# Local attention: which engine reads the projected rows first, and what stands behind it in each queue

## The chip, the cores and the metric

One Trainium2 chip, one of its cores. The metric is the device time of one execution in microseconds (us), smaller is better. The engines are TensorE (PE, with its weight loads as PEld), VectorE (DVE), ScalarE (ACT), GpSimd (POOL) and SyncE (SP). Each takes its instructions in the order of its own queue, and waits for the others on semaphores.

## The reference, cut to what matters

The whole program is two layers of a small network over 16 sequences of 256 tokens with 128 features: linear attention, experts, a retention block, and last a stack of two local attention layers, each with a feed-forward part. The change touches the local attention alone:

```python
h = shift_token(x)
q, k, v = jnp.split(h @ wqkv, 3, axis=-1)          # 8 heads of 64
q = l2norm(q) * qs;  k = l2norm(k) * ksc
q, k = rotary_xpos(q, k)                           # each row times cos and sin tables
sim = jnp.einsum('bhwid,bhwjd->bhwij', bq * 8.0, bk)   # windows of 64, looking one window back
sim = jnp.where(mask, -jnp.finfo(sim.dtype).max, sim)
attn = jax.nn.softmax(sim, axis=-1)
out = jnp.einsum('bhwij,bhwjd->bhwid', attn, bv)
x = x + out @ wo
```

## The kernel before, in words

`local_layer` is called twice. Its attention part works on eight chunks of 512 tokens (two sequences), each of four tiles of 128 tokens. A *step* holds four tiles of projection for chunk g, most of the scores and values of chunk g - 1, and the last ones with the output product of chunk g - 2. A step has eight *blocks*, `blk` 0 to 7, and every engine walks through the same blocks in an order written out by hand in its own `step` function. The first step of a layer only projects, the second projects and attends, six do all three, and two more drain. The six run as three rounds of a hardware loop of two steps.

In an even block, for tile t:

- PE, `project_qk` (L1410): q into bank BA and k into bank BB, three matmuls each. It waits until ACT has copied the turned rows of an earlier tile out of the same two banks (`qk_r`).
- ACT, `squares` (L1561): the squares of both banks into `sq`. DVE, `rotate` (L1664): both banks times the tables, into `R`. DVE waits for the squares of a bank before it reads that bank, so ACT always reads first and DVE last, and `rotated` is the semaphore that tells PE that a bank may be overwritten.
- DVE, `lengths` (L1671, L1674): row sums of `sq`, clipped. ACT, `norms` (L1566, L1569), the last thing in ACT's even block: logarithm and exponential of the sums, the reciprocal lengths `rn`.
- POOL (L1385, L1392): adds the two halves of the rotation and multiplies by `rn`. 

In an odd block PE projects v into BA (L1419) and turns the rows of the tile before (`turn`, L1436) into BB and BA. ACT copies v (`keep_values`, L1590), and later the turned rows (`keep_rows`, L1577 and L1584).

Every block also carries one pair of heads through four stages, each a block or two behind the other: `maxima_scores` on PE (L1450, L1454) and `maxima` on DVE (L1683, L1685); `scores` with `less_maxima` (L1471 to L1486) and ACT's `weights` (L1601); `weighted_values` (L1498, L1499); ACT's `denominators` (L1607, L1609) and DVE's `normalise` (L1694). `maxima_scores` may overwrite its banks only when DVE has read the pair before (`max_r`). Twice in a step, in blocks 2 and 6, PE turns the collected maxima (L1505), ACT copies them (`maxima_rows`, L1595, tile `mT`), and `less_maxima` waits for the copy; in these two blocks PE issues `maxima_scores` behind `less_maxima`, in the others ahead of `scores`. In block 4 PE forms the output product of chunk g - 2 in bank BB (`output`, L1515), and in block 6 DVE writes the shifted input rows of the next chunk (`shift_chunk`, L1647 to L1651).

Of the kernel before, what the change touches and what calls it, by code (L numbers as in the profile page):

```python
# [1292 lines left out]
def need(eng, sem, value):  # L1293

    if not isinstance(value, int) or value > 0:
        eng.wait_ge(sem, value)


def local_layer(k, l, shared):
# [5 lines left out]
    with ExitStack() as big:  # L1305
# [4 lines left out]
        with ExitStack() as ctx:  # L1310
# [36 lines left out]
            def staged(g, par, project, attend, finish, blk, lag):  # L1347


                p = blk - lag  # L1350
                if p >= 0:
                    return (g - 1, 1 - par, p) if attend else None
                return (g - 2, par, p + NPAIR) if finish else None
# [43 lines left out]
            def _(pe):  # L1397
                pe.wait_ge(zeroed, 4 * L)

                def project_qk(g, par, t, attend):  # L1400
                    n = NTILE * g + t
                    if not attend:
                        need(pe, rotated, 2 * n)
                        need(pe, v_sb, n)
                    if t == 0:
                        pe.wait_ge(shifted, g + 1 + l)
                    need(pe, qk_r, 2 * n - 2)
                    for qk, bank in enumerate((BA, BB)):
                        for wp, hp in PASSES:
                            m = nc.tensor.matmul(ps[bank][:], hs[hp][par][:, t * P:(t + 1) * P],  # L1410
                                                 k.lw["wqkv"][wp][:, qk * INNER:(qk + 1) * INNER],
                                                 start=(wp + hp == 0), stop=(wp == 1))
                        m.then_inc(proj, 1)

                def project_v(g, par, t):
                    n = NTILE * g + t
                    pe.wait_ge(rotated, 2 * n + 1)
                    for wp, hp in PASSES:
                        m = nc.tensor.matmul(ps[BA][:], hs[hp][par][:, t * P:(t + 1) * P],  # L1419
                                             k.lw["wqkv"][wp][:, 2 * INNER:3 * INNER], start=(wp + hp == 0), stop=(wp == 1))  # L1420
                    m.then_inc(v_mm, 1)

                def turn(c, t, project, written):
                    n = NTILE * c + t
                    for qk, bank in enumerate((BB, BA)):
                        if not project:
                            need(pe, qk_r, 2 * n)
                        elif bank == BA:
                            pe.wait_ge(v_sb, n + 2)
                        elif written is not None:  # L1430
                            pe.wait_ge(resid, written + 1)
                        else:
                            pe.wait_ge(rotated, 2 * n + 4)
                        pe.wait_ge(normed, 2 * n + 1 + qk)
                        for b in range(NB):
                            m = nc.tensor.transpose(ps[bank][:, b * P:(b + 1) * P], R[:, t % 2, qk, 0, b * P:(b + 1) * P],  # L1436
                                                    k.const["ident"][:])
                        m.then_inc(turned, 1)
# [67 lines left out]

                def output(c, par, n):
                    if n is not None:
                        pe.wait_ge(rotated, 2 * n + 2)
                    else:  # L1510
                        pe.wait_ge(qk_r, 2 * NTILE * (c + 1))
                    pe.wait_ge(o_r, NPAIR * (c + 1))
                    pe.wait_ge(w_in, L * 16 * len(names))
                    for b in range(NB):
                        i = nc.tensor.matmul(ps[BB][:], w["wo2"][:, b, :], OT[par][:, b, :], start=(b == 0), stop=(b == NB - 1))  # L1515
                    i.then_inc(x_mm, 1)
# [34 lines left out]
            def _(act):  # L1551
# [4 lines left out]
                def squares(g, t):  # L1556
                    n = NTILE * g + t
                    for qk, bank in enumerate((BA, BB)):
                        act.wait_ge(proj, 2 * n + qk + 1)
                        need(act, clipped, n)  # L1560
                        nc.scalar.activation(sq[:, qk, :], ps[bank][:], ACT.Square).then_inc(squared, 1)  # L1561

# [23 lines left out]
                def keep_values(g, par, t):  # L1586
                    act.wait_ge(v_mm, NTILE * g + t + 1)
                    if t % 2 == 0:
                        need(act, av_mm, NU * (g - 2) + NPAIR * (t // 2 + 1))
                    nc.scalar.activation(VA[par][:, t, :, 0:DH], ps[BA][:].rearrange("p (h d) -> p h d", d=DH),  # L1590
                                         ACT.Copy).then_inc(v_sb, 1)
# [19 lines left out]
                def step(g, par, project, attend, finish):  # L1611
                    now = (g, par, project, attend, finish)
                    for blk in range(2 * NTILE):
                        t = blk // 2
                        if project and blk % 2 == 0:
                            squares(g, t)
                        if project and blk % 2:
                            keep_values(g, par, t)
                        rows = turned_at(g, par, project, attend, blk)
                        if attend and blk in (2, 6):  # L1620
                            maxima_rows(g - 1, blk // 4)
                        dn = staged(*now, blk, 4)
                        if dn:
                            denominators(dn[0], dn[2])
                        sc = staged(*now, blk, 2)
                        if sc:
                            weights(sc[0], sc[2])
                        if blk % 2 and rows:
                            keep_rows(*rows)
                        if project and blk % 2 == 0:  # L1630
                            norms(g, t)
# [4 lines left out]
            def _(dve):  # L1636
# [20 lines left out]
                def rotate(g, t):  # L1657
                    n, i = NTILE * g + t, t % 2
                    for qk, bank in enumerate((BA, BB)):
                        dve.wait_ge(squared, 2 * n + qk + 1)  # L1660
                        need(dve, turned, 2 * n - 3 + qk)
                        x = ps[bank][:].rearrange("p (o h d) -> p o h d", o=1, d=DH).to_broadcast([P, 2, HEADS, DH])
                        y = tab[:, qk, 2 * (t % SPC):2 * (t % SPC) + 2, :].rearrange("p c (o d) -> p c o d", o=1)
                        nc.vector.tensor_tensor(R[:, i, qk, :, :].rearrange("p c (h d) -> p c h d", d=DH), x,  # L1664
                                                y.to_broadcast([P, 2, HEADS, DH]), ALU.mult).then_inc(rotated, 1)

                def lengths(g, t):
                    n, i = NTILE * g + t, t % 2
                    dve.wait_ge(squared, 2 * n + 2)
                    need(dve, rnorm, n - 1)  # L1670
                    nc.vector.tensor_reduce(ss[:, i, :], sq[:].rearrange("p q (h d) -> p (q h) d", d=DH), AX.X,  # L1671
                                            ALU.add).then_inc(sums_r, 1)
                    dve.wait_ge(sums_r, n + 1)
                    nc.vector.tensor_scalar(ss[:, i, :], ss[:, i, :], CLIP2, None, ALU.max).then_inc(clipped, 1)  # L1674
# [37 lines left out]
                def step(g, par, project, attend, finish):  # L1712
                    now = (g, par, project, attend, finish)
                    for blk in range(2 * NTILE):
                        t = blk // 2
                        if project and blk % 2 == 0:
                            rotate(g, t)
                            lengths(g, t)
                        if finish and blk == 5:
                            add_output(g - 2)  # L1720
                        mx = maxima_at(g, project, attend, blk)
                        if mx:
                            maxima(*mx)
                        if attend and blk in (1, 5):
                            split_maxima(g - 1, blk // 4)
                        nr = staged(*now, blk, 4)
                        if nr:
                            normalise(*nr)
                        if project and blk == 6:
                            need(dve, v_mm, NTILE * g)  # L1730
                            shift_chunk(g + 1, 1 - par)
# [242 lines left out]
```

## Time and profile before

| | |
|---|---|
| median of 3 runs | 1837.03 us (1834.8 to 1840.29) |
| the profiled execution's own time | 1841.57 us |
| its span, first to last instruction | 1839.8 us |
| PE busy over the span | 1376.4 us (75%) |
| DVE busy | 1167.5 us (63%) |
| ACT busy | 930.9 us (51%) |
| POOL busy | 723.3 us (39%) |

The span is from the first instruction of the program to the last. Matmuls are pipelined, so busy PE is not PE at its peak. The attention of the first layer runs from 845 to about 1233 us of the span, that of the second from 1341 to 1731 us. The shares are means over stages with different limits; what counts for the change is what each engine waits for inside those two stretches.

### The profile page before, as it was taken

Reading aid. Unit: us, or ns where it says so; the run is one execution under the profiler, and the core shown is the slowest. Engines: PE = TensorE matmul, PEld = TensorE weight load, DVE = VectorE, ACT = ScalarE, POOL = GpSimd, SP = SyncE. Lnnn points to the kernel's source line nnn. Section 1 sums busy time; section 2 is a strip of 40 time slices with the busy share of each in tenths; the row PEclk is TensorE's granted clock in tenths of the full one; section 3 lists DMA queues with packets and bytes.
Section 4 is the critical chain, followed back from the end, with each engine's and each line's share of the span. In section 5 each row is a group of like instructions: output and inputs, shape, how many; then the busy total and the mean of one; then the engine's idle time right before and its main releaser. Section 6 shows DMA issues by size and latency. Waiting matters only on the chain. (4 is left out here: it accounts for less than half of the span.)

```text
span 1839.8 us, 24389 instructions
## 1 busy us (share of the span) xinstructions
PE 1376.4 (75%) x6912; PEld 875.6 (48%) x6912; DVE 1167.5 (63%) x2605; ACT 930.9 (51%) x1749; POOL 723.3 (39%) x588
## 2 busy tenths in 40 slices
PE   7745564674539993874788888888858888889887
PEld 3312121243428872322566666663336666667533
DVE  1598898338448881535777777744467777777444
ACT  6411111344315550563577777764336777777543
POOL 0287787116653664224444333301054444443000
PEclk9867776876769995986899999999958999999999
DMA  5400000012121214000000000000000000000001
GB/s 157 151 0 0 0 0 0 0 47 72 44 62 49 77 47 132 6 0 18 1 1 2 1 1 1 1 26 0 16 2 1 1 2 0 1 0 0 1 0 46
DMA packets 50658, 44.44 MB, mean 24 GB/s; under 512 B 5870, under 2 KB 43763, under 8 KB 50560
## 3 DMA queue, kind: packets, MB, share of 16 engines
q1 hardware_dynamic: 45952, 34.91, 6.5%
q0 software_dynamic: 4608, 8.47, 1.4%
q8 instruction: 32, 0.52, 0.1%
q14 instruction: 66, 0.54, 0.1%
HBM read 23.28 MB, written 21.12 MB: 24 GB/s over the span
## 5 line engine op out<-in xcount | busy, mean ns | idle before, releaser
L1385 POOL TENSOR_TENSOR R<-R 128x512 f32<-128x512 f32 x128 | 159.4, 1267 | 393.6 <-DVE R L1664 393.6
L1664 DVE TENSOR_TENSOR R<-bank,tab 128x1024 f32<-128x1024 f32 x128 | 151.7, 1220 | 138.9 <-ACT sq L1561 133.7
L1392 POOL TENSOR_TENSOR R<-R,rn 128x512 f32<-128x512 f32 x128 | 133.9, 1068 | 12.1 <-issue 10.0
L1498 PE MATMUL bank<-PT,VA 128*128 128x192 f32 x512 | 131.5, 339 | 0.0
L1694 DVE TENSOR_TENSOR OT<-bank,rd 64x256 f32<-64x256 f32 x256 | 106.3, 415 | 18.2 <-ACT rd L1609 16.5
L1034 POOL DMA_INDIRECT expert_rows<-Yt,xin x80 | 82.5, 1031 | 80.2 <-DVE Yt L1007 58.2
L1561 ACT ACTIVATE sq<-bank 128x512 f32<-128x512 f32 x128 | 76.3, 598 | 63.3 <-PE bank L1410 57.4
L1601 ACT ACTIVATE PT<-bank 128x320 f32<-128x320 f32 x256 | 98.0, 435 | 18.3 <-PE bank L1486 13.8
L395 PE MATMUL bank<-phk,spread 128*128 128x512 f32 x64 | 45.8, 880 | 77.8 <-DVE phq L445 77.8
L463 DVE TENSOR_TENSOR_SCAN S<-beta,U 128x512 f32<-128x512 f32 x64 | 102.0, 1603 | 1.1
L1683 DVE CUSTOM_DVE_ANT_0 masked<-bank,mask_q 128x128 bf16<-128x128 f32 x256 | 73.8, 288 | 43.1 <-PE bank L1454 31.7
L1410 PE MATMUL bank<-wqkv_hi,hs_hi 128*128 128x512 f32 x128 | 63.2, 493 | 48.5 <-DVE hs_lo L1651 38.4
L1499 PE MATMUL bank<-PT,VA 128*128 128x128 f32 x512 | 98.9, 275 | 0.0
L1499 PEld LDWEIGHTS bank<-PT,VA 128*128 128x128 f32 x512 | 91.2, 192 | 0.0
L1685 DVE CUSTOM_DVE_ANT_0 masked<-bank,mask_q 128x192 bf16<-128x192 f32 x256 | 90.2, 352 | 0.1
L1450 PE MATMUL bank<-QKr 64*128 64x128 f32 x256 | 42.8, 331 | 60.2 <-DVE nm L1685 60.2
L1607 ACT ACTIVATE rd<-bank 64x512 f32<-64x512 f32 x128 | 76.1, 594 | 16.8 <-PE bank L1499 14.0
L1498 PEld LDWEIGHTS bank<-PT,VA 128*128 128x128 f32 x512 | 79.7, 194 | 9.5 <-issue 6.7
L1609 ACT ACTIVATE rd<-rd 64x512 f32<-64x512 f32 x128 | 80.7, 631 | 4.1
L1436 PE MATMUL bank<-ident,R 128*128 128x128 f32 x512 | 77.2, 298 | 6.0 <-ACT VA L1590 5.7
L723 POOL DMA_INDIRECT expert_slots<-tok_rows,dst x64 | 64.9, 1014 | 42.1 <-DVE tok_rows L832 23.8
L423 ACT ACTIVATE lden<-bank,deps 128x512 f32<-128x512 f32 x16 | 11.0, 687 | 133.2 <-PE bank L403 133.2
(306 smaller groups left out, 3946.1 us busy)
## 6 DMA issues: line engine op xcount, KB each, us to landing
expert_slots<-empty SPq DMA_DIRECT2D x8, 650.0 KB, 6.5
xin<-expert_slots SPq DMA_DIRECT2D x8, 650.0 KB
expert_rows<-empty SPq DMA_DIRECT2D x8, 512.0 KB, 6.7
Ye<-expert_rows SPq DMA_DIRECT2D x16, 256.0 KB, 5.0
expert_raw<-w1e_dram SPq DMA_DIRECT2D x9, 256.0 KB, 2.8
expert_raw<-w2e_dram SPq DMA_DIRECT2D x9, 256.0 KB, 2.9
tok<-x_dram SPq DMA_DIRECT2D x8, 256.0 KB, 4.4
out_dram<-tok_out SPq DMA_DIRECT2D x8, 256.0 KB, 2.7
```

The source lines that it names most:

```text
L463: nc.vector.tensor_tensor_scan(S[i % 2][:], beta[m][:, chunk(c)], U[d][:], 0.0, ALU.mult, ALU.add).then_inc(s_scan, 1)
L1034: nc.gpsimd.indirect_dma_start(k.ys[:, :], bass.IndirectOffsetOnAxis(ap=ids, axis=0), Yt[:, s % 3, t, :], None, bounds_check=2 * T - 1, oo ...
L1385: nc.gpsimd.tensor_tensor(halves[:, :, 0, :, z, :], halves[:, :, 0, :, z, :], halves[:, :, 1, :, 1 - z, :], ALU.add).then_inc(summed, 1)
L1392: nc.gpsimd.tensor_tensor(x, x, scale.to_broadcast([P, HEADS, DH]), ALU.mult).then_inc(normed, 1)
L1436: m = nc.tensor.transpose(ps[bank][:, b * P:(b + 1) * P], R[:, t % 2, qk, 0, b * P:(b + 1) * P], k.const["ident"][:])
L1498: nc.tensor.matmul(bank[:, o:o + KW], VA[par][:, 2 * s, h, :], pt[:, 0:KW], start=True, stop=True)
L1499: nc.tensor.matmul(bank[:, o + P:o + SEQ], VA[par][:, 2 * s + 1, h, :], pt[:, KW:KW + P], start=False, stop=True, skip_group_check=True).t ...
L1601: nc.scalar.activation(PT[:, u % 4, :], ps[BT + u % 2][:, 0:KW + P], ACT.Exp, scale=QK_SCALE).then_inc(pt_r, 1)
L1609: nc.scalar.activation(rd[:, p % 2, :], rd[:, p % 2, :], ACT.Exp, scale=-1.0).then_inc(rd_r, 1)
L1664: nc.vector.tensor_tensor(R[:, i, qk, :, :].rearrange("p c (h d) -> p c h d", d=DH), x, y.to_broadcast([P, 2, HEADS, DH]), ALU.mult).then_ ...
L1685: nc.vector.tensor_tensor_reduce(masked[:, v % 2, KW:2 * KW], bank[:, KW:2 * KW], mask[:, KW:2 * KW], -1.0, FAR, ALU.add, ALU.min, nm[:, 2 ...
L1694: m = nc.vector.tensor_tensor(OT[par][i * DH:(i + 1) * DH, b, s * SEQ:(s + 1) * SEQ], ps[BO + p % 2][0:DH, i * SEQ:(i + 1) * SEQ], rd[:, p ...
```

## The change

Each bank is now read first by DVE's rotation, which waits for the projection (`proj`), and then by ACT's squares, which wait for `rotated`. PE, which overwrites the banks, waits for `squared` where it waited for `rotated`. POOL's wait is unchanged. On DVE the row sums stand behind the block's maxima. On ACT the denominators of an even block stand ahead of the squares, and with that ahead of `maxima_rows`.

```diff
 project_qk (PE)
-                        need(pe, rotated, 2 * n)
+                        need(pe, squared, 2 * n)
 project_v (PE)
-                    pe.wait_ge(rotated, 2 * n + 1)
+                    pe.wait_ge(squared, 2 * n + 1)
 turn (PE)
-                            pe.wait_ge(rotated, 2 * n + 4)
+                            pe.wait_ge(squared, 2 * n + 4)
 output (PE)
-                        pe.wait_ge(rotated, 2 * n + 2)
+                        pe.wait_ge(squared, 2 * n + 2)
 squares (ACT)
-                        act.wait_ge(proj, 2 * n + qk + 1)
+                        act.wait_ge(rotated, 2 * n + qk + 1)
 step (ACT)
                         t = blk // 2
+                        dn = staged(*now, blk, 4)
+                        if dn and blk % 2 == 0:
+                            denominators(dn[0], dn[2])
                         if project and blk % 2 == 0:
                             squares(g, t)
...
                         if attend and blk in (2, 6):
                             maxima_rows(g - 1, blk // 4)
-                        dn = staged(*now, blk, 4)
-                        if dn:
+                        if dn and blk % 2:
                             denominators(dn[0], dn[2])
 rotate (DVE)
-                        dve.wait_ge(squared, 2 * n + qk + 1)
+                        dve.wait_ge(proj, 2 * n + qk + 1)
 step (DVE)
                             rotate(g, t)
-                            lengths(g, t)
                         if finish and blk == 5:
                             add_output(g - 2)
                         mx = maxima_at(g, project, attend, blk)
                         if mx:
                             maxima(*mx)
+                        if project and blk % 2 == 0:
+                            lengths(g, t)
```

## Rows read from the trace of the kernel before

**Rows 1.** Page, costliest groups: busy and mean ns, idle before, releaser
```profile
L1450 PE MATMUL bank<-QKr 64*128 64x128 f32 x256 | 42.8, 331 | 60.2 <-DVE nm L1685 60.2
```

**Rows 2.** Table of windows, one full step: window, length, each engine's busy time
```profile
core 0: us, PE busy (x) PEld busy (x) DVE busy (x) ACT busy (x) POOL busy (x), PEclk, DMA share, GB/s
...
969.20:1013.60 44.40, 39.77 (x305) 30.29 (x304) 34.84 (x107) 33.24 (x70) 18.35 (x16) 1.00 0.01 2
```

**Rows 3.** Waits, 845 to 1250 us: total, times, longest
```profile
DVE R L1664 <- ACT sq L1561: 67.8, 28, 5.3
```

**Rows 4.** Timeline of DVE: start, duration, instruction, idle before and releaser
```profile
964.76 0.72 DVE L1647 TENSOR_SCALAR hs_hi<-H 64x512 fp32r x1
...
967.40 0.69 DVE L1651 TENSOR_TENSOR hs_lo<-H,hs_hi 64x510 fp32r<-64x510 f32 x1
...
969.97 2.35 DVE L1664 TENSOR_TENSOR R<-bank,tab 128x1024 f32<-128x1024 f32 x2
...
979.72 2.36 DVE L1664 TENSOR_TENSOR R<-bank,tab 128x1024 f32<-128x1024 f32 x2 [1.55 <-ACT sq L1561]
981.99 1.21 DVE L1671 TENSOR_REDUCE ss<-sq 128x16 f32<-128x1024 f32 x1
...
983.48 0.29 DVE L1683 CUSTOM_DVE_ANT_0 masked<-bank,mask_q 128x128 bf16<-128x128 f32 x1
...
984.46 0.84 DVE L1694 TENSOR_TENSOR OT<-bank,rd 64x256 f32<-64x256 f32 x2
...
998.30 0.29 DVE L1683 CUSTOM_DVE_ANT_0 masked<-bank,mask_q 128x128 bf16<-128x128 f32 x1 [1.83 <-PE bank L1454]
```

**Rows 5.** Timeline of ACT, blocks 2 and 3 of the same step
```profile
979.00 1.30 ACT L1561 ACTIVATE sq<-bank 128x512 f32<-128x512 f32 x2
980.19 0.27 ACT L1595 ACTIVATE mT<-bank 128x128 bf16<-128x128 bf16 x1
980.49 0.59 ACT L1607 ACTIVATE rd<-bank 64x512 f32<-64x512 f32 x1
...
981.77 0.77 ACT L1601 ACTIVATE PT<-bank 128x320 f32<-128x320 f32 x2
983.50 0.21 ACT L1566 ACTIVATE ss<-ss 128x16 f32<-128x16 f32 x1 [0.96 <-DVE ss L1674]
...
986.65 1.09 ACT L1577 ACTIVATE QK<-bank 128x512 f32<-128x512 f32 x2
```

**Rows 6.** Timeline of PE, matmuls, second step and two full steps
```profile
889.76 0.47 PE L1450 MATMUL bank<-QKr 64*128 64x128 f32 x2 [2.71 <-DVE nm L1685]
...
968.24 0.50 PE L1410 MATMUL bank<-wqkv_hi,hs_hi 128*128 128x512 f32 x1 [0.82 <-DVE hs_lo L1651]
...
978.01 0.48 PE L1410 MATMUL bank<-wqkv_hi,hs_hi 128*128 128x512 f32 x1
...
980.68 0.23 PE L1484 MATMUL bank<-mT,sel 128*128 128x128 bf16 x1
...
981.07 0.33 PE L1450 MATMUL bank<-QKr 64*128 64x128 f32 x2
...
984.60 0.33 PE L1450 MATMUL bank<-QKr 64*128 64x128 f32 x2 [0.78 <-DVE nm L1685]
...
987.80 0.49 PE L1410 MATMUL bank<-wqkv_hi,hs_hi 128*128 128x512 f32 x1
...
991.92 3.70 PE L1515 MATMUL bank<-OT,wo 128*128 128x512 f32 x8 [0.82 <-DVE R L1664]
...
997.64 0.33 PE L1450 MATMUL bank<-QKr 64*128 64x128 f32 x2
...
1001.16 0.50 PE L1410 MATMUL bank<-wqkv_hi,hs_hi 128*128 128x512 f32 x1
...
1012.10 0.49 PE L1410 MATMUL bank<-wqkv_hi,hs_hi 128*128 128x512 f32 x1 [0.82 <-DVE hs_lo L1651]
...
1023.44 0.50 PE L1410 MATMUL bank<-wqkv_hi,hs_hi 128*128 128x512 f32 x1
...
1033.55 0.50 PE L1410 MATMUL bank<-wqkv_hi,hs_hi 128*128 128x512 f32 x1
```

## The prediction

> **What bounds the kernel now.** I began with the page: TensorE (PE) is the busiest engine, and the row with the largest stall of PE in the attention is the one in which its score matmuls for the maxima wait for VectorE (DVE), 60.2 us over both layers [rows 1]. The table of windows for one full step (a chunk projected, the one before attended, the one before that finished) shows PE busy for 39.77 of 44.40 us at the full clock [rows 2], so at most 4.6 us of a step can be won by taking waits away. There are six such steps in each of the two layers, twelve in all. The waits of the first layer say what the change aims at: DVE's rotation waits 67.8 us for ACT's squares [rows 3].
>
> I then read the timelines of DVE, ACT and PE through one step. Work comes in pairs of blocks: the even block projects q and k, the odd one v. I measure from PE's start on the q projection. Pair 0/1 takes 978.01 - 968.24 = 9.77 us, pair 2/3 takes 987.80 - 978.01 = 9.79 (in every second step 1033.55 - 1023.44 = 10.11), pair 4/5, with the output product in it, 1001.16 - 987.80 = 13.36, pair 6/7 1012.10 - 1001.16 = 10.94 [rows 6]. The sum is 43.9 to 44.2.
>
> What closes the loop of a pair is to be seen in pair 2/3 [rows 4 to 6]. From PE's start at 978.01: q is projected and squared at 979.00 (+0.99), DVE rotates q and k from 979.72 to 981.99 (2.27 for the two), makes the row sums until 983.48 (1.49), reads the maxima until 984.46 (0.98). Two things wait on that. PE takes up its next maxima scores at 984.60, 0.78 late. But ACT's logarithm of the row sums starts at 983.50, as soon as DVE has clipped them, and everything ACT does in the odd block is queued behind it: v's copy, denominators, weights, and the copies of the turned rows, which start at 986.65 and take 1.09. Their end, 987.74, is what PE's next q projection waits for, since they empty the two banks: it starts at 987.80. So two chains, one through the maxima and one through the norms, end within 0.1 us of each other. ACT needs 987.80 - 983.50 = 4.30 from the norms to the next projection, and I take 4.22 of it as its own (the weights in it start up to 0.08 late, for PE).
>
> **The change part by part.** No instruction is added or taken away; four orders change. (1) Rotation no longer waits for the squares. It gains 979.72 - 979.00 = 0.72 us wherever DVE is free. (2) The row sums go behind the maxima: 0.98 later for the norms, 1.49 earlier for the maxima. (3) The squares go behind the rotation, and what follows them in ACT's queue with them: in blocks 2 and 6 the copy of the turned maxima (mT), then the weights in each even block. (4) PE's waits move from rotated to squared, and ACT takes the denominators first. Net of (1) and (2), the norms come 0.98 - 0.72 = 0.26 later in the best case, and ACT's chain, which had no slack, is longer by that before (3) is counted. What PE gains on the maxima it can't use: it arrives early at the next projection and waits for the emptied banks.
>
> *Pair 2/3 after*, from PE's start at 0. ACT's denominators begin when the row copies end, at about 1.0, and take 981.77 - 980.49 = 1.28: until 2.28. DVE rotates q and then k from 0.99 on, and 2.36 later k is written: 3.36. ACT squares k at 3.40, and mT follows 0.49 behind (980.19 against the second square, 0.70 behind 979.00) and takes 0.27: ready at 4.17. PE wants it at 980.68 - 978.01 = 2.67 and gets it at 4.22: 1.55 late. In this block the maxima's scores are issued behind it (981.07 - 980.68 = 0.39 on): 4.61; DVE sees them 998.30 - 997.64 = 0.66 later, 5.27 [rows 4, 6]. Maxima until 6.25, row sums until 7.74, norms at 7.77, and 4.22 more to the next projection: 11.99. That is +2.20 in half the steps and +1.88 in the others; I take 2.04.
>
> *Pair 6/7 after.* The same until 7.74. Behind the row sums DVE has the normalising (0.84, and 0.04 to the next) and the shifted rows of the next chunk, 964.76 to 968.09 = 3.33 in one piece [rows 4]: 11.95, and PE begins 0.14 later, 12.09, against 10.94: +1.15. Before, too, PE waited 0.82 there for exactly these rows [rows 6].
>
> *Pair 0/1 after.* DVE comes late from the shift: before, it rotated at 969.97, 1.73 after PE's start; after the change the same work (maxima, normalising) lies between, so again 1.73. The rotation gains nothing from (1) here. 1.73 + 2.27 + 0.98 + 1.49 = 6.47, norms at 6.50, next projection 10.72: +0.95.
>
> *Pair 4/5 after.* PE's output product starts at 991.92, 4.12 after PE's start, having waited for the rotation of k; it would now wait for the square of k, done at 4.0. Everything later hangs on this product and on v behind it, and ACT waits there anyhow. I take 0. This is the one place where the later squares could cost what is cheap to bound: between -0.1 and +0.5 (one square).
>
> Sum for a full step: 0.95 + 2.04 + 0 + 1.15 = 4.14 us; twelve steps: 49.7.
>
> *The other steps.* The first step of a layer has no attention; rotation, squares and sums stand in one line either way: 0. In the second, the last three pairs pay as above, without output (0.2 to 0.4 + 2 + 1.15, less because the slow clock covers some: 2.8), and the first pair has a wait of 2.71 us for the maxima [rows 6] of which I give back half: +1.4. In the drain step ACT has no squares, but its denominators (1.28) now stand ahead of mT twice: between 0 and 2.6, I take 1.3. Together 2.7 per layer, 5.4.
>
> Total +55. The profiled execution took 1841.57 us with a span of 1839.8, and the median is 1837.03, so the profile stands for it within 0.3%; that is also about what a measurement of this kernel can tell from no change. 1837 + 55 = **1892 us**.
>
> A rule of the Trainium skill speaks for the change: Perfetto Trace Analysis, section Optimization Strategies, says that where the matmul engine idles for other engines, those that block it are to be improved. By that rule the 60.2 us of [rows 1] are the prize, and the sum would be about 1837 - 60 = 1777. The trace does not show that this prize can be collected: the second chain, through the norms and the row copies, ends 0.1 us from the first.
>
> **The rivals.**
> *Faster: the maxima are the bound.* If PE's waits for the maxima set the pace alone, they go (-60.2) and a little comes back: 1777 to 1810. For it: the size of the wait. Against it: PE is ready and the row copies are not, at 987.74 against 987.80. It decides if ACT's queue from norms to row copies has 0.3 us or more to spare in pairs 0/1 and 2/3. 7 in 100.
> *No change.* The gains on the maxima and the losses on the norms cancel, which needs mT not to be late in blocks 2 and 6, by the denominators and squares finding an earlier place than I gave them: 1831 to 1843. Against it: the square of k can't precede the rotation of k, whose end at 3.36 is later than PE's need at 2.67. 5 in 100.
> *Slower, but by the norms only.* If mT's delay is swallowed (PE would otherwise stand in the odd block), the sum is 0.26 to 0.95 a pair, 2.2 to 2.9 a step, 26 to 35 in all with the edges: 1863 to 1875. 12 in 100.
> *Slower, and the clock falls.* PE's share falls from 90% to 39.8 / 48.5 = 82% of a full step, in stalls of about 1.5 us. If the granted clock dropped to half for a tenth of the time, PE's work would grow by some 4 us in a step, 48 in all: about 1940. The row shows it at full at 90% [rows 2]; no row of mine shows it at 82. 6 in 100.
> *The forecast*, 70 in 100, on its own 1876 to 1910.
>
> **How the numbers follow.** The range goes from the norms-only case to a little above the forecast's own: 1863 to 1912. The two cases beneath 1863 hold 12 in 100, the clock 6. The latencies between engines (0.03 to 0.14 in each hand-over) occur about eight times in a chain and could move a pair by 0.4, hence plus or minus 18 us around the sum. Chances: faster 0.07, same 0.05, slower 0.88.
>
> **What will show it.** Right, if pair 2/3 takes close to 12.0 and pair 6/7 close to 12.1, pair 0/1 10.7, pair 4/5 still 13.4; if PE hardly waits for the maxima of the odd blocks, but waits for mT in blocks 2 and 6 by about 1.5 us and, before the q projections of pairs 0/1 and 2/3, for the row copies by 1 to 1.5 us; if DVE's wait for the squares is gone and a wait of ACT's squares for the rotation stands in its place. The prediction is wrong in its step on ACT if the norms are later and the row copies are not; in its step on mT if PE takes mT up within 3 us of its start. A changed duration of the rotation or the squares, now that their order on a bank is turned, would be something that I left out.

## The result, and the profile after

The changed kernel takes 1914.35 us (median of 4 runs, 1912.11 to 1921.39), the kernel before 1838.66 on the same chip: a ratio of 1.0409, with a 95% interval of 1.038 to 1.0437. It is slower, as forecast, but by 75.7 us where 55 were predicted, and 2.4 us above the end of the range. The profiled execution took 1912.11 us, with a span of 1910.2 against 1839.8.

The page of the kernel after, costliest groups (busy and mean ns, then idle time before and its releaser):

```profile
L1666 DVE TENSOR_TENSOR R<-bank,tab 128x1024 f32<-128x1024 f32 x128 | 151.9, 1221 | 112.4 <-PE bank L1410 103.5
...
L1561 ACT ACTIVATE sq<-bank 128x512 f32<-128x512 f32 x128 | 76.4, 597 | 106.1 <-DVE R L1666 102.8
L1410 PE MATMUL bank<-wqkv_hi,hs_hi 128*128 128x512 f32 x128 | 63.9, 499 | 83.2 <-DVE hs_lo L1653 46.2
```

The rotation's wait for the squares [rows 3] is gone, and a wait of the squares for the rotation stands in its place. The wait of [rows 1], PE for the maxima, fell too. The same group of the kernel after has what is left of the 60.2 us:

```profile
L1450 PE MATMUL bank<-QKr 64*128 64x128 f32 x256 | 44.1, 341 | 3.2 <-DVE nm L1687 3.0
```

So the largest wait of PE shrank by 57 us and the program became some 75 us longer. Where PE waits instead is in its timeline through one full step (start, duration, instruction, idle before and releaser), to be read beside [rows 6]:

```profile
1072.92 0.49 PE L1410 MATMUL bank<-wqkv_hi,hs_hi 128*128 128x512 f32 x1 [1.80 <-DVE hs_lo L1653]
...
1083.90 0.50 PE L1410 MATMUL bank<-wqkv_hi,hs_hi 128*128 128x512 f32 x1 [1.23 <-ACT QK L1577]
...
1088.20 0.23 PE L1484 MATMUL bank<-mT,sel 128*128 128x128 bf16 x1 [1.55 <-ACT mT L1595]
...
1095.90 0.50 PE L1410 MATMUL bank<-wqkv_hi,hs_hi 128*128 128x512 f32 x1 [1.23 <-ACT QK L1577]
...
1109.27 0.50 PE L1410 MATMUL bank<-wqkv_hi,hs_hi 128*128 128x512 f32 x1
...
1121.86 0.49 PE L1410 MATMUL bank<-wqkv_hi,hs_hi 128*128 128x512 f32 x1 [1.82 <-DVE hs_lo L1653]
```

PE waits 1.23 us for the row copies ahead of the projections that end pairs 0/1 and 2/3, 1.55 us for mT, and 1.8 us for the shifted rows (0.82 in [rows 6]). The table of windows gives the step as 49.00 us with 40.06 of PE's work, at the full clock, against 44.40 and 39.77 in [rows 2]:

```profile
core 0: us, PE busy (x) PEld busy (x) DVE busy (x) ACT busy (x) POOL busy (x), PEclk, DMA share, GB/s
1072.90:1121.90 49.00, 40.06 (x303) 30.18 (x303) 35.72 (x106) 33.08 (x71) 18.32 (x16) 1.00 0.00 1
```

ACT's timeline, blocks 2 and 3 of this step, beside [rows 5]: denominators, the squares, the second of them held by the rotation, mT, and the norms after a wait of 2.29 us.

```profile
1084.90 0.59 ACT L1607 ACTIVATE rd<-bank 64x512 f32<-64x512 f32 x1
...
1086.25 0.60 ACT L1561 ACTIVATE sq<-bank 128x512 f32<-128x512 f32 x1
1087.38 0.60 ACT L1561 ACTIVATE sq<-bank 128x512 f32<-128x512 f32 x1 [0.53 <-DVE R L1666]
1087.87 0.27 ACT L1595 ACTIVATE mT<-bank 128x128 bf16<-128x128 bf16 x1
...
1091.68 0.22 ACT L1566 ACTIVATE ss<-ss 128x16 f32<-128x16 f32 x1 [2.29 <-DVE ss L1676]
...
1094.75 1.09 ACT L1577 ACTIVATE QK<-bank 128x512 f32<-128x512 f32 x2
```

The pairs, from PE's start on one q projection to the next, medians over the full steps of both layers, worked out from PE's timeline:

| pair | before | predicted | after |
|---|---|---|---|
| 0/1 | 9.82 | 10.72 | 10.97 |
| 2/3 | 9.79 | 11.99 | 12.05 |
| 4/5 | 13.37 | 13.36 | 13.36 |
| 6/7 | 10.95 | 12.09 | 12.61 |

The span, cut at the first q projection of a chunk, both layers together: start of the attention -6.1 (front part, untouched), first steps +2.7, second steps +6.7, the stretch of full steps up to the last pair 6/7 +53.1, this pair and the drain to the last matmul of the output product +8.6, what stands behind it in each layer (the feed-forward part above all, no code of which changed) +5.5. Before rounding the sum is +70.4, which is the difference of the spans.

What I had left out is in two timelines of the kernel after. First DVE, then POOL:

```profile
1079.16 0.48 DVE L1676 TENSOR_SCALAR ss<-ss 128x16 f32<-128x16 f32 x1
...
1081.53 0.93 DVE L1710 CAST hl<-nm 128x16 bf16<-128x16 f32 x1
...
1117.83 1.26 DVE L1649 TENSOR_SCALAR hs_hi<-H 64x512 fp32r x1
1119.10 1.17 DVE L1650 TENSOR_SCALAR hs_hi<-H 64x510 fp32r x1
```

```profile
1077.10 2.51 POOL L1385 TENSOR_TENSOR R<-R 128x512 f32<-128x512 f32 x2 [6.03 <-DVE R L1666]
...
1080.39 2.04 POOL L1392 TENSOR_TENSOR R<-R,rn 128x512 f32<-128x512 f32 x2 [0.78 <-ACT rn L1569]
...
1117.77 2.22 POOL L1392 TENSOR_TENSOR R<-R,rn 128x512 f32<-128x512 f32 x2 [2.48 <-ACT rn L1569]
```

Take the ends, each a start and a duration added up. The clip ends at 1079.64, POOL's additions at 1079.61. The cast ends at 1082.46, POOL's multiplications at 1082.43. The second of the two copies into `hs_hi` ends at 1120.27, POOL's second multiplication at 1119.99. A clip of 16 numbers a row takes 0.17 us elsewhere in the trace; here it ends 0.03 us after what POOL had begun before it. I take it that DVE is held by POOL (the run with POOL's work in quarters, below, shows it), and that I read such lengthened durations of the trace before (0.72 for the first copy, [rows 4]) as costs of the instructions. The other way round, POOL's second multiplication beside these copies takes 1.22 us, where one takes 1.04 elsewhere.

The Trainium skill has this in SBUF — State Buffer, sections "SBUF: two separate sides" and "Who interferes with whom": of a pair of memory ports that VectorE shares with GpSimd, the instruction that starts first keeps it whole, and the other engine's stands still; copies, casts and tensor_scalar are among VectorE's instructions that can take this pair, a row sum is not on trn2. The ends above agree with it to 0.03 us for the clip (a tensor_scalar) and the cast, and the row sums kept their duration (1216 ns on average, 1208 before).

### The profile page after: what moved, and what is told of

The parts are those of the page before. It is cut to its first block and busy times, and to the rows that moved or that the text cites. A ratio compares the mean times of both kernels' runs of the same rounds, so it can differ in the third digit from the quotient of the medians.

```text
span 1910.2 us, 24389 instructions
## 1 busy us (share of the span) xinstructions
PE 1410.5 (74%) x6912; PEld 892.0 (47%) x6912; DVE 1193.1 (62%) x2605; ACT 928.6 (49%) x1749; POOL 722.6 (38%) x588
## 5 line engine op out<-in xcount | busy, mean ns | idle before, releaser
L1666 DVE TENSOR_TENSOR R<-bank,tab 128x1024 f32<-128x1024 f32 x128 | 151.9, 1221 | 112.4 <-PE bank L1410 103.5
L1498 PE MATMUL bank<-PT,VA 128*128 128x192 f32 x512 | 136.6, 350 | 0.0
L1499 PE MATMUL bank<-PT,VA 128*128 128x128 f32 x512 | 102.9, 284 | 0.0
L1499 PEld LDWEIGHTS bank<-PT,VA 128*128 128x128 f32 x512 | 95.8, 200 | 0.0
L1498 PEld LDWEIGHTS bank<-PT,VA 128*128 128x128 f32 x512 | 82.3, 200 | 9.8 <-issue 7.2
L1484 PE MATMUL bank<-mT,sel 128*128 128x128 bf16 x256 | 48.1, 227 | 43.9 <-ACT mT L1595 43.8
L1673 DVE TENSOR_REDUCE ss<-sq 128x16 f32<-128x1024 f32 x64 | 77.8, 1216 | 4.0 <-ACT sq L1561 4.0
```

The costliest lines, as they stand in the source:

```text
L1498: nc.tensor.matmul(bank[:, o:o + KW], VA[par][:, 2 * s, h, :], pt[:, 0:KW], start=True, stop=True)
L1499: nc.tensor.matmul(bank[:, o + P:o + SEQ], VA[par][:, 2 * s + 1, h, :], pt[:, KW:KW + P], start=False, stop=True, skip_group_check=True).t ...
```

## The experiments

Theory A is the prediction's: in-order queues, in which the norms stand ahead of everything that ACT does in an odd block, and mT behind the squares. Theory B, its rival: PE's clock, or the extra stalls as such. Theory L came from the profile after: DVE held by POOL. The order here is that of the argument. Each ratio is to the kernel before on the same chip; diffs are against the kernel after, or before where it is said. Pairs are medians as above.

**mT ahead (e2_mt_first).**

```diff
 step (ACT)
                         t = blk // 2
+                        if attend and blk in (2, 6):
+                            maxima_rows(g - 1, blk // 4)
                         dn = staged(*now, blk, 4)
...
-                        if attend and blk in (2, 6):
-                            maxima_rows(g - 1, blk // 4)
```

> The changed kernel with ACT's copy of the turned maxima (mT) moved ahead of the denominators and squares, nothing else. Theory A: pair 2/3 goes from 12.0-12.5 to about 10.5, pair 6/7 from 12.6 to 11.0-11.4, pairs 0/1 (11.0) and 4/5 (13.4) stay. Full step about 46.0: total about 1872, PE's wait for mT (43.8 us by the page) is gone. Rival A' (the 0.98 us of sums behind maxima are the whole of it and mT's delay is swallowed later): total stays over 1900. Rival B (clock): gains only as far as the half-speed windows go away.

Measured: 1.0125 (1.0098 to 1.0153), 1850.69 us. Pairs 10.97, 10.39, 13.37, 10.97. Pairs 2/3 and 6/7 give back 1.66 and 1.64 us, and 0/1, which has no mT in it, stands where it was. mT's place behind the squares, and so behind the rotation, made about two thirds of the loss: 4.09 - 1.25 = 2.84 of 4.09%.

**Lengths ahead of the maxima again (e1_sums_first).**

```diff
 step (DVE)
                             rotate(g, t)
+                            lengths(g, t)
...
-                        if project and blk % 2 == 0:
-                            lengths(g, t)
```

> The changed kernel with one part undone: DVE's row sums ahead of the maxima again (rotation first, denominators first and the squares behind the rotation stay). Theory A (the chain through the norms sets the pace, made longer by the 0.98 us of the maxima ahead of the sums, and in blocks 2 and 6 by the late mT copy in front of those maxima): the sums then wait only for the square of k (about 4.0 us after PE's start), norms at about 5.5, so pairs 0/1 and 2/3 come to about 10.4 and 10.4 (from 11.0 and 12.0 to 12.5), 6/7 to 10.9 to 11.4 (from 12.6), 4/5 stays 13.4. Full step 45.1 to 45.6 instead of 49.1: total about 1860. PE still waits 1.5 us for mT in blocks 2 and 6. Rival B (the time is lost to the granted clock, which falls because PE stalls): the stalls for mT stay, so most of the loss stays, over 1890. Rival C (the order of the readers on a bank makes rotation or squares slower): nothing changes, 1914.

Measured: 1.0299 (1.0268 to 1.033), 1882.14 us. Pairs 11.70, 11.56, 13.36, 11.12. In the places that ran at the full clock, pair 0/1 took 10.30 to 10.97 and pair 2/3 10.88, where A expects 10.4 for both; most others had a stretch at half clock in them, and took 12.1 to 14.09. Here is the wait ahead of one such pair in PE's timeline, and an example of such a stretch from the table of windows of the same kernel:

```profile
1063.14 0.33 PE L1450 MATMUL bank<-QKr 64*128 64x128 f32 x2 [1.64 <-DVE nm L1687]
```

```profile
1050.00:1053.40 3.40, 3.40 (x15) 2.27 (x15) 3.34 (x13) 1.66 (x4) 2.04 (x2) 0.53 0.00 0
```

A expected some 1860, a ratio of about 1.012, so this is a miss of it: with the lengths in front, PE waits 1.64 us for the maxima and 1.55 for mT, and the half-clock stretches of B come on top. A is off at the full clock too: it has the norms at about 5.5 us after PE's start, and by ACT's timeline they begin at 6.08 in pair 2/3 and 6.73 in pair 0/1 (medians). The clip takes 0.60 to 0.68 us there, beside POOL's additions, where it took 0.23 before.

**Both (e3_mt_and_sums_first).** The two diffs above together, so that only the order of the readers and the denominators of the change are left.

> Both edits of the two kernels before: mT ahead, row sums ahead of the maxima. What stays of the change is the rotation ahead of the squares and the denominators ahead of them. Theory A: pairs about 10.4, 9.8, 13.4, 10.9: full step 44.5 against 43.9 of the kernel before, total 1842 to 1850. If the parts are not additive because another wait stands behind (mT's copy hides the sums or the other way), the total lies over 1860.

Measured: 1.0237 (1.0198 to 1.0276), 1868.98 us. Pairs 12.51, 10.37, 13.36, 11.14. A's forecast, 1842 to 1850, is missed by 19 us or more. The kernel is worse than e2_mt_first alone, and nearly all of it in pair 0/1. PE's timeline and two windows of that step:

```profile
1060.27 0.33 PE L1450 MATMUL bank<-QKr 64*128 64x128 f32 x2 [1.85 <-DVE nm L1687]
```

```profile
1052.50:1061.20 8.70, 6.54 (x47) 4.88 (x49) 7.83 (x25) 5.04 (x12) 3.71 (x4) 0.96 0.00 1
1061.20:1064.60 3.40, 3.40 (x25) 3.17 (x24) 1.98 (x12) 2.22 (x5) 0.83 (x1) 0.60 0.00 0
```

PE stands 1.85 us for the maxima, and behind it comes a stretch with a granted clock of 0.60, most of it at the lower of the two levels (1.2 and 2.4 GHz). It comes at the same place of nearly every step: at 965, 1013, 1061, 1108 and 1160 us in the first layer, at 1439, 1487, 1535, 1583 and 1631 in the second. The one full step without it has 10.95 in this pair, so by this one step it costs 12.51 - 10.95 = 1.6 us. That it comes from PE's wait is not shown. In the kernel after, PE's waits come at other places, and the pair medians have none of it. What the second part of the change, lengths behind the maxima, earns is this: with mT ahead it is worth 2.37 - 1.25 = 1.1%. Without the stretch e3 would be no better than e2 either, for a reason that neither theory had. Two groups of DVE in e3:

```profile
L1673 DVE TENSOR_REDUCE ss<-sq 128x16 f32<-128x1024 f32 x64 | 78.1, 1220 | 53.1 <-ACT sq L1561 53.1
L1676 DVE TENSOR_SCALAR ss<-ss 128x16 f32<-128x16 f32 x64 | 34.4, 538 | 2.2
```

In the kernel before, the row sums waited for nothing and the clip took 240 ns on average. Here k is squared only after its rotation, the sums wait 53.1 us in all for that, and the clip runs beside POOL's additions; with the lengths in front, all of it lies on the way to the maxima, and PE's wait for them is 78.6 us on the page's count where it was 60.2 before.

**The second part alone (e5_sums_behind_alone).** The kernel before, with the lengths behind the maxima:

```diff
 step (DVE), against the kernel before
                             rotate(g, t)
-                            lengths(g, t)
...
                             maxima(*mx)
+                        if project and blk % 2 == 0:
+                            lengths(g, t)
```

> The kernel before with one part of the change done alone: DVE's row sums behind the maxima. ACT's squares still come first and mT is in time. Theory A (two chains of equal length; the norms' chain has no slack, so 0.98 us more in it shows in full, and PE's earlier maxima give nothing back): pairs 0/1 10.7-11.0 (9.8 before), 2/3 10.7 (9.8), 4/5 13.4, 6/7 10.9-11.4 (10.9). Full step +2.3 us: ratio to the kernel before about 1.015. PE's wait for the maxima (60 us by the page) nearly gone. Rival (the maxima are the bound and the sums a side branch): the same wait gone and the ratio below 0.99.

Measured: 1.0212 (1.0174 to 1.025), 1882.52 us against 1843.2. Pairs 11.17, 10.95, 13.37, 11.53. Slower than the 1.015 that I expected of A: the later lengths bring the clip beside POOL's additions (0.48 us for 0.23), the later norms bring POOL's multiplications beside the cast and the copies (the shift takes 3.89 us for 3.33). So by itself this edit loses on the norms what it wins on the maxima, and more.

**Denominators at their old place (e6_den_behind).**

```diff
 step (ACT)
-                        dn = staged(*now, blk, 4)
-                        if dn and blk % 2 == 0:
-                            denominators(dn[0], dn[2])
...
-                        if dn and blk % 2:
+                        dn = staged(*now, blk, 4)
+                        if dn:
                             denominators(dn[0], dn[2])
```

> The changed kernel with ACT's denominators back behind the squares and the mT copy, as in the kernel before. Theory A: the denominators' place is worth nothing in the full steps, since ACT waits for the rotation anyway in front of the squares and for the sums behind them (1.3 to 2.3 us each): ratio to the kernel before 1.037 to 1.045, as the change itself (1.041). If they did harm ahead of mT (drain step) it is up to 0.2% lower; if they filled a hole that is now missing, higher.

Measured: 1.0399 (1.0369 to 1.043), 1898.98 us against 1826.42. Pairs 10.97, 12.11, 13.37, 12.62, those of the kernel after. Their place is worth nothing that can be told: ACT would stand at that point for the rotation anyhow. Nor is it in the drain, which with the last pair 6/7 took 54.6 and 54.7 us here, 53.4 and 54.9 in the kernel after.

**POOL's multiplications in quarters (e8_scale_in_quarters).** The same work in four instructions of 128x128 for each of 128x512, so that POOL lets DVE in between.

```diff
-  nc.gpsimd.tensor_tensor(x, x, scale.to_broadcast([P, HEADS, DH]), ALU.mult).then_inc(normed, 1)
+  for h in range(0, HEADS, 2):
+      m = nc.gpsimd.tensor_tensor(x[:, h:h + 2, :], x[:, h:h + 2, :],
+                                  scale[:, h:h + 2, :].to_broadcast([P, 2, DH]), ALU.mult)
+  m.then_inc(normed, 1)
```

> The changed kernel with POOL's multiplication by the reciprocal lengths cut into four instructions of 128x128 for each of 128x512. It tests a term that the forecast lacked: in the changed kernel DVE's single-source copies and clips end within 0.05 us of the end of the POOL instruction that runs beside them (first shifted copy 1.26 us instead of 0.72, the cast of the maxima 0.93, the clip 0.48 instead of 0.23). Theory L (DVE is held until the running POOL instruction ends): with POOL's multiplications about 0.27 us each the first shifted copy takes 0.5 to 0.8 us, pair 6/7 goes from 12.6 to about 12.1, the total 5 to 8 us down. Rival (the slow copy has another cause, such as code loading): the copy stays at 1.26 and nothing changes, or the extra instructions cost time.

Measured: 1.0261 (1.023 to 1.0292), 1894.33 us against 1843.2. Pairs 10.44, 12.05, 13.37, 12.11. The answers for the line of the copies, first of the kernel after, then of this one (smallest, median and largest duration in ns):

```profile
L1649 DVE TENSOR_SCALAR hs_hi<-H x18: 409/1264/1299, 836.9 to 1748.8; 64x512 fp32r x12, 64x512 fp32r<-64x512 f32 x6
```

```profile
L1652 DVE TENSOR_SCALAR hs_hi<-H x18: 408/621/659, 837.9 to 1737.8; 64x512 fp32r x12, 64x512 fp32r<-64x512 f32 x6
```

The median copy fell from 1.26 to 0.62 us, and pair 6/7 from 12.61 to 12.11. No instruction of DVE was touched. That POOL holds DVE is shown by this: cut the holder into pieces, and the held one gets short. The gain is larger than the 5 to 8 us that I expected: the pairs make 1.0 us in a step, 12 in all, and the ratio fell by 1.5%, some 27 us; the rest was not taken apart. The four pairs now add up to 47.97 us; I had predicted 10.72 + 11.99 + 13.36 + 12.09 = 48.16. That they agree so well is partly luck. The shift takes 2.78 us here, less than the 3.33 of the forecast, so the rotation of pair 0/1 begins 1.21 us after PE's start and not 1.73, and the pair stays under its forecast though its clip, beside POOL's additions, which were not cut, still takes 0.48. And pair 6/7 is now set by the norms, as pair 2/3 is, and not by the shift that the forecast had there.

**The shifted rows two blocks earlier (e4_shift_early).**

```diff
 step (DVE)
-                        if project and blk == 6:
+                        if project and blk == 4:
                             need(dve, v_mm, NTILE * g)
                             shift_chunk(g + 1, 1 - par)
```

> The changed kernel with the next chunk's shifted rows made by DVE in block 4 (behind its other work there) instead of block 6. Theory A: DVE's 3.33 us no longer stand between the late row sums of pair 6 and PE's next projection, nor in front of the rotation of pair 0: pair 6/7 goes from 12.6 to 12.0 (the norms' chain), pair 0/1 from 11.0 to 10.0-10.3, 4/5 to 13.4-13.8, 2/3 unchanged. Full step 47.5: total about 1893. Rival: if the shift is not in the way, pairs 6/7 and 0/1 stay and the total is 1914 or more, since DVE's output addition in block 5 comes later.

Measured: 1.0291 (1.0264 to 1.0318), 1878.47 us. Pairs 10.32, 12.13, 13.44, 12.01. As expected: the shift is what pairs 6/7 and 0/1 pay above A's norms, and pair 4/5, which PE and its output product set, takes it for 0.08 us.

**The norms behind the row copies (e7_norms_late).** If the fault is that the norms stand ahead of ACT's odd block, they can stand behind it.

```diff
 step (ACT)
                         if blk % 2 and rows:
                             keep_rows(*rows)
-                        if project and blk % 2 == 0:
+                        if project and blk % 2:
                             norms(g, t)
```

> The changed kernel with ACT's norms taken out of the way: they stand at the end of the odd block, behind the copies of the turned rows, instead of at the end of the even block. Nothing on ACT then waits for the row sums before PE's banks are emptied. Theory A (the norms in ACT's queue carry the loss, besides mT and the shift): pair 0/1 9.0-9.5 (11.0), 2/3 10.6 (12.0-12.5, mT still 1.5 us late), 4/5 13.4, 6/7 12.1-12.6 (12.6): full step 45.1-45.7, ratio to the kernel before 1.010 to 1.017 instead of 1.041. Rival (POOL's multiplication, which then comes 4 us later, becomes the wait of the turns): PE waits for R in the odd blocks and little is won, over 1.03.

Measured: 0.991 (0.9881 to 0.9939), 1827.45 us against 1843.2. Pairs 8.98, 10.89, 13.37, 10.99. Better than expected (1.010 to 1.017), and the timeline of DVE says why:

```profile
998.90 0.42 DVE L1649 TENSOR_SCALAR hs_hi<-H 64x512 fp32r x1
999.34 0.42 DVE L1650 TENSOR_SCALAR hs_hi<-H 64x510 fp32r x1
...
1000.50 0.69 DVE L1653 TENSOR_TENSOR hs_lo<-H,hs_hi 64x510 fp32r<-64x510 f32 x1
```

POOL multiplies at another time, the copies take 0.42 us each, and the shift from first to last 2.3 us, where it took 3.33 before and 3.87 after the change. The first step of a layer falls from 38.4 us to 27.2 and 30.8, presumably since there the norms were in the way of the v copy, too. What is left in PE's timeline is the wait for mT:

```profile
994.65 0.23 PE L1484 MATMUL bank<-mT,sel 128*128 128x128 bf16 x1 [1.55 <-ACT mT L1595]
```

**mT ahead and norms behind (e9_mt_first_norms_late).** The diffs of e2 and e7.

> The changed kernel with mT first (as in the run that did this alone) and with the norms behind the row copies. Theory A: both chains that the change lengthened are cut, and what it wins on the maxima can be used: pairs 9.0-9.3, 8.8, 13.4, 10.6-11.0: full step 41.8-42.5 against 43.9 before, ratio to the kernel before 0.985 to 0.992, faster than both. Rival (ACT's own load of 8.7 us a pair plus its waits is the bound): pairs 0/1 and 2/3 over 9.7 and the ratio 1.00 or more.

Measured: 0.9626 (0.9596 to 0.9656), 1773.11 us against 1843.2. Pairs 8.99, 9.26, 13.37, 9.38. That is over 2% better than A's range, for the reason seen in e7: pair 6/7, expected at 10.6 to 11.0, has the shift at 2.3 us in it. A full step takes 41.00 us with 39.41 of PE's work in it:

```profile
947.10:988.10 41.00, 39.41 (x303) 30.11 (x303) 33.25 (x106) 32.62 (x71) 18.09 (x16) 1.00 0.01 2
```

**Is it the norms alone? (e11_norms_late_before, e12_norms_late_sums_behind).** The kernel before with the norms moved as in e7; and the same with the lengths behind the maxima as well. In both, ACT's squares still read the banks first.

```diff
 step (ACT), against the kernel before; e12 has e5's edit on DVE too
                         if blk % 2 and rows:
                             keep_rows(*rows)
-                        if project and blk % 2 == 0:
+                        if project and blk % 2:
                             norms(g, t)
```

> The kernel before (squares first, sums ahead of the maxima) with ACT's norms behind the row copies, nothing else. Theory A with two chains of equal length: cutting the norms' chain alone leaves PE's wait for the maxima, so pairs 0/1 and 2/3 stay at 9.6-9.8 and PE's wait of about 60 us stays. What falls is POOL's collision with the shifted rows, whose multiplication comes later (pair 6/7 10.9 to 10.2), and the first step of a layer, which is one chain (37 to about 27 us): ratio 0.975 to 0.985. Rival (the norms alone set the pace): pairs 0/1 and 2/3 at 9.0, ratio under 0.97.

> The kernel before with two edits: row sums behind the maxima and norms behind the row copies. ACT's squares are still the first reader of each bank and mT is where it was. It shows what rotation before squares is worth once the norms are out of the way, against the run with mT first and norms late (0.963). Theory A: the reading order is worth nothing, as DVE's rotation ends 0.7 us later but nothing late hangs on it: pairs 9.0-9.2, 9.1-9.4, 13.4, 9.4-9.8, ratio 0.960 to 0.970. Rival (the earlier rotation is what paid): pairs 0/1 and 2/3 at 9.6 or more, ratio over 0.975.

Measured: e11 0.9957 (0.9939 to 0.9974), 1818.47 us, pairs 10.14, 10.15, 13.76, 10.28. e12 0.9731 (0.9702 to 0.976), 1778.11 us, pairs 8.93, 9.28, 13.76, 10.31. The first is a miss by over 1%: the chain through the norms is gone, but the one through the maxima holds PE alone, as the waits of its first layer show (total, times, longest; the kernel before has 30.2, 24, 2.7):

```profile
PE bank L1450 <- DVE nm L1685: 32.5, 24, 2.6
```

Pairs 0/1 and 2/3 came out longer than before (9.82 and 9.79), not as long. The norms now stand ahead of the next block's squares: these begin 1.37 us after PE's start (medians), where pair 2/3 before had 0.98, and the rotation behind them at 2.07 instead of 1.70. With the lengths behind the maxima (e12) most of that wait goes as well: the page's count for both layers is 68.7 us in e11 and 9.7 in e12. The two chains of the prediction are both there, and each hides the other: moving the lengths alone made 1.0212, moving the norms alone 0.9957, both together 0.9731. The ratio of e12 lies between the range of theory A (to 0.970) and that of its rival (over 0.975). Against e9 it still lacks 0.9731 - 0.9626 = 1.05%. The third difference between them, the place of the denominators, was worth nothing in e6, so this is what the rotation ahead of the squares, with mT ahead of both, brings: in pair 4/5 (13.76 to 13.37) and in pair 6/7 (10.31 to 9.38). In pair 4/5 it can be followed: with the squares first, late norms push the squares and the rotation back (to 2.11 us after PE's start, 1.09 in e9). So the reading order is worth something once the norms are late, against what A expected.

**The best version (e10_best_shift_early).** The diffs of e2, e7 and e4.

> mT first and norms late, and besides the shifted rows made in block 4. Theory A: pair 0/1 loses its late rotation (9.0 to 8.7-8.9), 6/7 goes to about 9.2, 4/5 13.4-13.5, 2/3 9.3. PE, busy 39.8 us of 40.6, is then the bound: ratio 0.953 to 0.963. Rival (block 5 suffers: output addition and maxima behind 3 us of shift): 4/5 at 14 or more and no gain on 0.963.

Measured: 0.9577 (0.9552 to 0.9603), 1748.67 us against 1826.42. Pairs 8.93, 9.26, 13.36, 9.28. It is within A's range; its interval touches that of e9, so the gain over e9, 0.5%, is not certain.

```profile
1000.00:1041.00 41.00, 39.70 (x304) 30.23 (x303) 33.49 (x106) 32.68 (x70) 18.02 (x16) 1.00 0.00 0
```

PE is busy for 39.70 of 41.00 us. Taking waits away has little more to give in a full step; the next gain would have to come from PE's own work.

## Why the prediction was right and where it was not

**Two chains that end together: right.** A change aimed at one of them moved the end to the other. e11 and e12 show it from both sides. The rule of the Trainium skill that I had weighed (Perfetto Trace Analysis, section Optimization Strategies: improve what blocks an idle matmul engine) led to 1777 us. The wait it points at did shrink, from 60.2 to 3.0 us, with the time going up by 4.1%; only with the norms moved does the kernel come near that figure (1773 in e9).

**mT behind the squares: right, in place and size.** Pair 2/3 was predicted at 11.99 and took 12.05, the wait for mT was predicted at 1.55 us and is 1.55, and e2 gives 1.66 of the 2.26 back.

**Pair 4/5 and the denominators at nothing: right** for the full step (13.36; e6). In the drain steps it was wrong to take 1.3 each for them: with the denominators at their old place (e6) the drains are no shorter. The last pair 6/7, which was in the steps' sum, and the drain cost 4.3 each where these terms make 2.45. In e2, with mT ahead, this stretch takes 51.6 and 51.5 us, against 49.9 before and 53.4 and 54.9 after, so about half of it or more is mT; the rest was not taken apart.

**Pair 6/7 and the clip of pair 0/1: the step that failed.** "Behind the row sums DVE has ... the shifted rows of the next chunk, 964.76 to 968.09 = 3.33 in one piece" took a duration from the trace before as a property of the instructions. It was the sum of 2.3 us of work and 1.0 us in which POOL held DVE, and the change, which moved the norms and so POOL's multiplications later, raised the hold to 1.6: the shift took 3.87, the pair 12.61 instead of 12.09. In pair 0/1 the clip went from 0.23 to 0.48 beside POOL's additions, the norms began at 6.75 instead of 6.50, and the pair came to 10.97 instead of 10.72. (The cast went to 0.93 as well, but the norms do not wait for it.) That is 0.52 + 0.25 = 0.8 us in a step, some 9 us in twelve. e8 shows the cause for the copies; for the clip it rests on the ends alone, since POOL's additions were not cut. The other terms held in the kernel after itself: norms at 7.78 for 7.77 in pair 2/3, and 4.22 from the norms to the next projection in pair 0/1.

**First and second steps: wrong.** Costed at 0, the first step of a layer took 1.4 us more each: "rotation, squares and sums stand in one line either way" overlooks that the clip in that line is held by POOL's additions: its four clips take 0.77, 0.75, 0.75 and 0.53 us, before 0.27 to 0.32. The second steps cost 6.7 together where I had 2.8: 2.0 in the second layer and 4.7 in the first, where pair 2/3 took 13.72 at a granted clock of 0.53 against 11.49 at 0.75.

Together, by segments, against the sum of 55: the stretch of full steps 53.1 - 47.4 = 5.7 more (the twelve terms without the two last pairs 6/7), first steps 2.7, second steps 3.9, drains 3.7, and the parts that the change does not touch -6.1 + 5.5 = -0.6. That is the 15.4 us by which the difference of the spans exceeds the forecast. The hold's 9 us show as 5.7 there because the mean full step of before was 1.1 us above its median pairs, and that of after 0.7. In both, pair 0/1 takes 1.5 us more in the first step of the second and third round of the hardware loop (11.34 for 9.8 before, 12.4 for 10.97 after); before, three of these four also have a half-clock stretch (12.88 to 13.41). The medians differ by 5 us more than the two profiled executions: that of after was 2.2 us under its median, that of before 2.9 above.

**The clock: a rival with more in it than its 6 in 100, though not what made this result.** In the full steps of the kernel after there are 13 stretches at half clock where before there were 3, but the mean step exceeds the sum of the median pairs by 0.7 us after and by 1.1 before, so they did not add to the difference there. Behind the attention they did. The table of windows for that part of the second layer, before and after:

```profile
1729.80:1839.80 110.00, 88.31 (x210) 36.35 (x208) 45.83 (x73) 46.37 (x64) 0.99 (x2) 0.95 0.07 19
...
1795.20:1910.20 115.00, 92.68 (x210) 38.23 (x208) 45.81 (x73) 46.36 (x64) 0.98 (x2) 0.90 0.07 18
```

The same code took 5.0 us more at a granted clock of 0.90 instead of 0.95, which is nearly all of the +5.5 of these parts. The clock there went up and down between the variants as well (108 to 115 us for a layer), so this is no price of the change that could be forecast; why it falls is open. In e1 and e3, where PE waits 1.6 to 1.9 us for the maxima in the same place of many steps, the half-clock stretches took about 1% of the whole, an estimate from their pairs with a stretch and without.

## What to carry to other kernels

When the largest wait of the busiest engine is to be removed, follow the second chain first: here both ended within 0.1 us, and only moving the short instructions that wait at the head of an in-order queue (the norms, 0.5 us of work ahead of an odd block's 4.2) let the gain be collected: with mT ahead as well, -3.7% instead of +4.1%. Before a duration is carried into a sum, look whether it ends with an instruction of another engine: a clip of 0.17 us that takes 0.48 is waiting, and its time will change when the other engine's work moves. Where a copy is wanted by the matmul engine at once, it stands ahead of work that waits for something later.

## What the runs showed of the hardware

DVE's copies, clip and cast are held by a POOL instruction that is under way when they begin: a copy of 0.42 us became 1.26, a cast of 0.17 became 0.93, a clip of 0.17 became 0.75. DVE's row sums (1216 ns, 1208 before) are not. The rotation and the squares kept their durations (1221 and 597 ns) with their order on a bank turned; which engine reads a bank first changes neither of them, and matters by what stands behind each in its queue. A wait of 1.85 us of PE in the same place of a step was followed, in nearly every step of e3, by a stretch at a granted clock of 0.60, worth some 1.6 us of the step; e2, where the row sums stand behind the maxima and that wait is gone, was 1.1% faster.
